# Row sums of the attention taken in halves of the queries, with four exponential buffers that change roles and one output buffer

## The reference

```python
h = layernorm(x) * (scale + 1) + shift          # shift, scale, gate from silu(cond) @ mod_w + mod_b
q, k, v = heads(h @ w_qkv)
q, k = rope(layernorm(q) * q_norm_w), rope(layernorm(k) * k_norm_w)
attn = softmax(q @ k.T / sqrt(32))
out = x + (concat_heads(attn @ v) @ w_out) * gate
```

## Time and profile before

| | |
|---|---|
| three runs | 1780.75, 1782.88 and 1783.54 us, median 1782.88 us |
| the profiled execution | 1788.56 us, its span 1786.7 us |
| TensorE clock granted, mean over the span | 0.980 of full speed |
| busy: PE, DVE, ACT, POOL | 94%, 70%, 58%, 36% of the span |
| chain that ended last | PE 85%, ACT 7%, DVE 5%, issue 2%, DMA 1% |
| main loop, tiles in flight (107 to 1637 us) | nearly all steps alike, 26.17 us in the one shown |

### The profile page before, as it was taken

One profiled execution on the slowest core, in us unless ns is written; L12 is line 12 of the kernel. 1 busy time (PEld: TensorE's weight loads), 2 busy tenths in 40 slices (PEclk: granted clock), 3 DMA queues, 4 the chain that ended last, 5 costly groups with the idle time before them and its releaser, 6 DMA issues.

```text
span 1786.7 us, 32167 instructions
## 1 busy us (share of the span) xinstructions
PE 1685.0 (94%) x12334; PEld 981.8 (55%) x12334; DVE 1243.3 (70%) x1605; ACT 1035.4 (58%) x1547; POOL 634.4 (36%) x707
## 2 busy tenths in 40 slices
PE   6978899999999999999999999999999999998777
PEld 3644455555555555555555555555555555554334
DVE  8766667767777776777777677777767777775443
ACT  3445656666666666666656656666665666665452
POOL 0513234334433433443343343334334333433222
PEclk9989999999999999999999999999999999999888
DMA  6034455546555564654546465464645546454544
GB/s 208 25 66 89 96 117 118 130 98 134 118 107 131 116 133 96 136 115 107 133 110 135 99 133 116 107 136 110 130 104 130 121 102 139 107 114 94 112 106 119
DMA packets 55566, 205.38 MB, mean 115 GB/s; under 512 B 6888, under 2 KB 6888, under 8 KB 39160
## 3 DMA queue, kind: packets, MB, share of 16 engines
q0 software_dynamic: 18288, 133.18, 39.0%
q1 hardware_dynamic: 37128, 70.14, 11.7%
HBM read 53.25 MB, written 16.88 MB: 39 GB/s over the span
## 4 chain that ended last, share of the span: by engine, by line
PE 85%; ACT 7%; DVE 5%; issue 2%; DMA 1%; SPq 0%; DVEq 0%; ACTq 0%
PE SA L413 13%; PE Y L325 11%; PE Y L338 10%; PE Y L328 9%; PE Y L332 9%; PE MB L441 7%; ACT probs L751 7%; PE O L432 7%; PE SM L381 7%; PE MB L360 3%; PE SA L417 3%; DVE cst L994 2%; PE SA L315 1%; PE SA L391 1%; PE SM L413 1%
## 5 line engine op out<-in xcount | busy, mean ns | idle before, releaser
L994 DVE TENSOR_REDUCE cst<-SM 128x2 fp32r<-128x1024 f32 x256 | 313.5, 1225 | 346.8 <-PE MB L381 346.8
L751 ACT ACTIVATE probs<-SM 128x1024 f32<-128x1024 f32 x256 | 262.0, 1023 | 242.1 <-PE SM L417 240.9
L1216 POOL DMA_DIRECT2D probs<-probs x127 | 110.2, 868 | 820.8 <-ACT probs L753 759.3
L994 DVE TENSOR_REDUCE cst<-MB 128x2 fp32r<-128x1024 f32 x256 | 311.4, 1217 | 0.0
L432 PE MATMUL O<-probs,vals 128*32 128x512 f32 x2048 | 278.1, 616 | 0.0
L753 ACT ACTIVATE probs<-SA 128x1024 f32<-128x1024 f32 x256 | 261.0, 1020 | 0.0
L651 ACT ACTIVATE rows<-Y 128x512 f32<-128x512 f32 x121 | 72.3, 597 | 268.0 <-PE Y L332 268.0
L325 PE MATMUL Y<-wqkv_hi,hT_hi 128*128 128x512 f32 x716 | 214.0, 420 | 0.0
L328 PE MATMUL Y<-wqkv_hi,hT_lo 128*128 128x512 f32 x716 | 193.1, 391 | 0.5 <-DVE hT_lo L976 0.5
L381 PEld LDWEIGHTS SM<-qk_hi 32*128 32x128 f32 x512 | 51.2, 183 | 258.9 <-issue 78.3
L332 PE MATMUL Y<-wqkv_lo,hT_hi 128*128 128x512 f32 x716 | 191.7, 389 | 0.0
(11 more groups left out here) (205 smaller groups left out, 3466.4 us busy)
## 6 DMA issues: line engine op xcount, KB each, us to landing
probs<-probs POOLq DMA_DIRECT2D x127, 1024.0 KB, 7.7
xin<-in_x_dram SPq DMA_DIRECT2D x62, 256.0 KB, 6.8
xres<-in_x_dram SPq DMA_DIRECT2D x60, 256.0 KB, 2.6
out_dram<-xres SPq DMA_DIRECT2D x60, 256.0 KB, 3.7
shift_scale<-mod_rows SPq DMA_DIRECT2D x15, 512.0 KB, 6.0
gate<-mod_rows SPq DMA_DIRECT2D x16, 256.0 KB, 5.2
rows<-in_L_cond_mod_w_dram SPq DMA_DIRECT2D x2, 1024.0 KB, 8.8
probs<-in_L_cond_w_qkv_dram SPq DMA_DIRECT2D x2, 1024.0 KB, 13.2
```

The source lines that it names most:

```text
L751: act.activation(probs[:, a, 2:4, :], SM[:], ACT.Exp).then_inc(s_exp, 1)
L994: dve.tensor_reduce(heads[:, 2 * half:2 * half + 2, 0], bank[:], AX.X, ALU.max, negate=True).then_inc(max_out, 1)
L1216: pool.dma_start(probs[:, probs_buffer(t - 1)].rearrange("p h n -> p (h n)"), probs[:, probs_buffer(t)].rearrange("p h n -> p (h n)"), acc ...
```

## The change

The exponentials get a fourth buffer, and which buffer a quarter uses alternates from group to group (`probs_buffer`). The products with ones are split into halves of 256 queries, and one half is done in each quarter, in front of `weigh_values`: of the first sum in quarter 3 and in quarter 0 of the next step, of the second in quarters 1 and 2 of the next step. They go to bank Y, between the projections, in place of MB, and the waits on PE, ACT and DVE follow. `log_sums`, `inverse_sums` and with them `scale_o` come a quarter later, `output_high` comes last in the step, and POOL's order changes. The outputs of all batch elements share one buffer in two layouts, so that a group of one element overwrites a tile of the last. `w_out` is loaded into the fourth exponential buffer, and its high and low parts are made ahead of the loop.

```diff
-    def probs_buffer(t):
-        return 1 if t % 2 else t
+    def probs_buffer(g, t):
+        return t ^ (g % 2)
...
-        probs = sb("probs", [P, 3, HG, T])
+        probs = sb("probs", [P, 4, HG, T])
...
-        oT = sb("oT", [P, 2, NG, T])
+        oT = sb("oT", [P, NG, TT, P])
...
-        wout_raw = oT[:, 1]
+        wout_raw = probs[:, 3]
...
+        def group_out(g):
+            return oT[:, :, g % NG, :] if (g // NG) % 2 else oT[:, g % NG, :, :]
+        def tile_out(n):
+            return oT[:, n % TT, :, :] if (n // TT) % 2 else oT[:, :, n % TT, :]
+        def half_cols(h):
+            return slice(h * T // 2, (h + 1) * T // 2)
...
-                if t == 1 and g >= 2:
-                    pe.wait_ge(sum_added, g - 1)
-                if t == 3 and g >= 1:
-                    pe.wait_ge(first_summed, g)
...
-            def add_over_keys(g, t, bank):
+            def add_over_keys(g, t, h):
                 pe.wait_ge(first_added if t == 0 else second_added, 16 * (g + 1))
+                if h == 1 or t == 2:
+                    pe.wait_ge(first_summed, 2 * g + (1 if t == 0 else 2))
+                if h == 1 and t == 2:
+                    pe.wait_ge(sum_added, 2 * g + 1)
+                if t == 0 and h == 0 and g > 0:
+                    pe.wait_ge(sum_added, 2 * g)
+                cols = half_cols(h)
                 for i in range(HG):
-                    mm = pe.matmul(bank[head_rows(i), :], ones_r[:, 0:E].bitcast(F32), probs[:, t, i, :],
+                    mm = pe.matmul(Y[head_rows(i), cols], ones_r[:, 0:E].bitcast(F32),
+                                   probs[:, probs_buffer(g, t), i, cols],
                                    start=True, stop=True, skip_group_check=True)
                 mm.then_inc(ones_done, 1)
...
                 scores_by_key(s, 0)
                 if s > 0:
+                    if tile(s + 5):
+                        pe.wait_ge(raw_out, raw_count(s + 5, 1))
+                    add_over_keys(s - 1, 0, 1)
                     weigh_values(s - 1, 3)
                 if group(s + 1):
                     scores_by_query(s + 1, 0)
                 if s > 0 and tile(s + 4):
-                    if tile(s + 5):
-                        pe.wait_ge(raw_out, raw_count(s + 5, 1))
-                    else:
-                        pe.wait_ge(y_gated, s - 5)
+                    pe.wait_ge(first_summed, 2 * s)
                     project(s + 4, 2, Y[:])
                 scores_by_key(s, 1)
                 if s > 0:
-                    if group(s + 1):
-                        pe.wait_ge(max_out, 2 * TT * (s + 1) + 2)
-                    add_over_keys(s - 1, 2, MB[:, 0, :])
+                    if tile(s + 4):
+                        pe.wait_ge(v_out, s + 5)
+                    add_over_keys(s - 1, 2, 0)
                 weigh_values(s, 0)
                 if group(s + 1):
                     scores_by_query(s + 1, 1)
...
                     if n == 0:
                         pe.wait_ge(wout_low, 1)
                     pe.wait_ge(o_low, n + 1)
-                    if tile(s + 4):
-                        pe.wait_ge(v_out, s + 5)
-                    else:
-                        pe.wait_ge(y_gated, n)
+                    pe.wait_ge(sum_added, 2 * s - 1)
                     project_out(n, Y[:], 0, 4)
                 if tile(s + 6):
                     transpose_x(s + 6)
...
                     project_out(n, Y[:], 4, 12)
                 scores_by_key(s, 2)
+                if s > 0:
+                    if n >= 0:
+                        pe.wait_ge(y_gated, n + 1)
+                    add_over_keys(s - 1, 2, 1)
                 weigh_values(s, 1)
                 if group(s + 1):
                     scores_by_query(s + 1, 2)
                 if tile(s + 6):
-                    if s - 5 >= 0:
-                        pe.wait_ge(y_gated, s - 4)
+                    if s > 0:
+                        pe.wait_ge(sum_added, 2 * s)
                     else:
                         pe.wait_ge(v_out, s + 5)
                     project(s + 6, 0, Y[:])
                 scores_by_key(s, 3)
                 if group(s + 1):
-                    pe.wait_ge(max_out, 2 * TT * (s + 1) + 6)
-                    add_over_keys(s, 0, MB[:, 0, :])
+                    if tile(s + 6):
+                        pe.wait_ge(raw_out, raw_count(s + 6, 0))
+                    add_over_keys(s, 0, 0)
                 weigh_values(s, 2)
                 if group(s + 1):
                     scores_by_query(s + 1, 3)
                 if tile(s + 6):
-                    pe.wait_ge(raw_out, raw_count(s + 6, 0))
+                    pe.wait_ge(first_summed, 2 * s + 1)
                     project(s + 6, 1, Y[:])
...
-                if g == NG:
-                    act.wait_ge(wout_low, 1)
-                if b > 1:
-                    act.wait_ge(o_low, TT * (b - 1))
-                act.activation(oT[:, b % 2, g % NG, :], O[:], ACT.Copy).then_inc(o_out, 1)
+                if b > 0:
+                    act.wait_ge(o_low, g - NG + 1)
+                act.activation(group_out(g), O[:].rearrange("p (t n) -> p t n", t=TT), ACT.Copy).then_inc(o_out, 1)
...
+            def move_first_sum(g, h):
+                act.wait_ge(ones_done, 4 * g + h + 1)
                 if g > 0:
                     act.wait_ge(o_scaled, g)
                 else:
                     act.wait_ge(parts_out, 3)
-                act.activation(sum_inv[:], MB[:, 0, :], ACT.Copy).then_inc(first_summed, 1)
+                cols = half_cols(h)
+                act.activation(sum_inv[:, cols], Y[:, cols], ACT.Copy).then_inc(first_summed, 1)
...
+                    if g > 0:
+                        act.wait_ge(pv_step, TT * (g - 1) + (t ^ 1) + 1)
                     if t == 0:
                         if g > 0:
-                            act.wait_ge(ones_done, 2 * g - 1)
+                            act.wait_ge(first_added, 16 * g)
                         else:
                             act.wait_ge(w_low[0], 1)
+                    elif t == 1:
+                        if g > 0:
+                            act.wait_ge(ones_done, 4 * g - 2)
+                        else:
                             act.wait_ge(w_low[1], 1)
-                    elif t == 1 and g > 0:
-                        act.wait_ge(pv_step, n - 1)
-                        act.wait_ge(second_added, 16 * g)
                     elif t == 2:
                         if g > 0:
-                            act.wait_ge(ones_done, 2 * g)
+                            act.wait_ge(second_added, 16 * g)
                         else:
                             act.wait_ge(mod_partial, 3)
                     elif t == 3:
-                        act.wait_ge(pv_step, n - 1)
-                        act.wait_ge(first_added, 16 * (g + 1))
-                a = probs_buffer(t)
+                        if g > 0:
+                            act.wait_ge(ones_done, 4 * g)
+                        else:
+                            act.wait_ge(wout_low, 1)
+                a = probs_buffer(g, t)
...
+            act.wait_ge(ld_wout, 16)
+            act.activation(wout_hi[:], wout_raw, ACT.Copy).then_inc(wout_high, 1)
...
                 key_exponentials(s, 0, 0)
+                if s > 0:
+                    move_first_sum(s - 1, 1)
                 key_exponentials(s, 0, 1)
+                if s > 0:
+                    move_o(s - 1)
                 if tile(s + 5):
                     square(s + 5, 1)
-                if s > 0:
-                    move_o(s - 1)
                 if s > 0 and tile(s + 4):
                     move_v(s + 4, Y[:])
                 key_exponentials(s, 1, 0)
                 key_exponentials(s, 1, 1)
-                if s > 0:
-                    log_sums(s - 1, sum_inv[:])
-                    inverse_sums(s - 1)
                 if tile(s + 6):
                     x_high(s + 6)
                 if tile(s + 5):
...
                 key_exponentials(s, 2, 0)
                 key_exponentials(s, 2, 1)
-                if s - 4 >= 0:
-                    output_high(s - 4)
-                if s == 1:
-                    act.wait_ge(ld_wout, 16)
-                    act.activation(wout_hi[:], wout_raw, ACT.Copy).then_inc(wout_high, 1)
+                if s > 0:
+                    log_sums(s - 1, sum_inv[:])
+                    inverse_sums(s - 1)
                 if tile(s + 6):
                     move_qk(s + 6, 0, Y[:])
                 key_exponentials(s, 3, 0)
                 if s < LAST:
-                    move_first_sum(s)
+                    move_first_sum(s, 0)
                 key_exponentials(s, 3, 1)
+                if s - 4 >= 0:
+                    output_high(s - 4)
...
+            def add_sums(g, h):
+                dve.wait_ge(ones_done, 4 * g + 3 + h)
+                dve.wait_ge(first_summed, 2 * g + 1 + h)
+                cols = half_cols(h)
```

(25 more changed lines are left out.)

64 lines of the change are left out of this document (30 added, 34 removed).

## The result

Over six runs of each kernel, the changed one takes 1788.79 us median (1787.44 to 1791.63), the one before 1782.92 (1780.75 to 1784.02): ratio 1.0031, 95% interval 1.0018 to 1.0043. It is slower by 0.3%; 1779.5 was forecast.

A forecast was written before the change was run, and what follows sets the result against it. PE was taken to bound the kernel, stopped by late exponentials. Held steps -1.6, ten free steps -5.5 and the end +4 gave -3: 1785.5 profiled, 5.7 lower for the median, stated as 1779.5 us; range 1753 to 1798.

The forecast's parts named there:

- The halves: Products with ones on PE: a half costs 0.46 us, a quarter 2.58, saving 0.55 us a step.
- the free step: Steps 1 to 4 and 57 to 62, without `normalize_x` and `add_residual` together: 25.62 us each.
- The rivals at 0.50 and 0.60: Dearer half products on PE: 0.50 us each gives 1786 us, chance 0.08; 0.60 gives 1800, chance 0.12.
- The place and time of the meeting: At a step's end DVE's `normalize_x` begins at 5.40 us after quarter 3's first matmul, inside POOL's `add_residual`.
- They take turns: DVE and POOL alternate whole instructions at a step's end: L960 ends at 6.57 us, `output_low` 7.71, L963 8.25.
- POOL is not interrupted: Rival: `output_low` also goes ahead of DVE's L960; DVE done at 8.60, step 26.49 us, total 1798, chance 0.10.
- the held step: Steps 5 to 56, where PE waits 0.52 us for `low_qk`: 26.14 us each, 0.03 below before.
- the way from L987 to PE's start: DVE work of 0.59 us, `low_qk` 1.41 and an assumed 0.1 for the semaphore: PE can go on at 10.35.
- PE's own arrival: PE itself would reach the next step's `scores_by_query` 9.83 us after quarter 3's first matmul.
- The term of -1.6: The 52 steps 5 to 56, at -0.03 us each.
- Free steps and end: Ten steps gain 0.55 us each, -5.5; in the last step `project_out(59)` waits 3.0 more, clock 3, taken as +4.
- The edits costed at nothing: Adding DMA, half copies, `add_sums`, `scale_o`, xres store, output parts and `w_out` copies: taken as covered, 0 us.

The follow-up runs named there:

- set_ahead: The changed kernel with a one-column memset, waited for, between POOL's adding DMA and `add_residual`: 1780.16 us, ratio 0.998 to the kernel before.
- wait_between: The changed kernel with one more wait on POOL, `output_low` waiting for the `add_residual` before it: 1771.41 us, ratio 0.993 to the kernel before.
- res_early: The changed kernel with `add_residual` moved from the end of POOL's step to ahead of the rotations: 1749.9 us, ratio 0.980 to the kernel before.

## Why the prediction failed

- **The halves: right.** 0.46 forecast, 0.46 and 0.45 measured (809.16 to 809.62, 828.18 to 828.63), and 0.456 in the mean of all from 250 to 1560 us; quarters 2.57 for 2.58, the free step 25.58 for 25.62. The rule of the Trainium skill, "TensorE: Matmul & The Clock Gate", section "Wait — 56ns, not 53.3ns?", would give 8 x 62 ns = 0.50; these rows give 57 ns a matmul and speak against its applying here. The rivals at 0.50 and 0.60 fall.
- **The place and time of the meeting: right, in part by luck.** From the first matmul of quarter 3 (827.04): exponentials done 3.48 (3.48 forecast), the DMA at 3.78 (3.92), `add_residual` done at 5.97 (6.02), L984 begun at 5.39 (5.40). But `add_residual` began 0.60 behind the DMA, not 0.82, and took 1.59, not 1.28: two errors that cancel. The 0.82 of the earlier trace rows was a wait. `scale_o` stood there until ACT had the inverse sum, at 818.80, and began 0.09 later:

```profile
818.17 0.63 ACT L726 ACTIVATE sum_inv<-sum_inv 128x512 f32<-128x512 f32 x1
```

- **"They take turns": this step failed.** L984 was to end at 6.57 and did at 7.76; `output_low` was to end at 7.71 behind it and did at 7.20 ahead of it; L987 was done at 8.55, not 8.25. This is the rival "POOL is not interrupted", given 0.10, which had 8.60. Its case against was rows 6 and 7; but there POOL's two instructions stand with a gap of 0.08 between them (87.93 + 0.73 to 88.74), far from a DMA, and in the code the second waits for the first's result (`rotate`). `set_ahead` shows that what decides is the DMA right in front, `wait_between` that a wait inside the pair undoes it. The row that would have warned was not in the trace of before: no such pair stood behind a DMA.
- **What that cost.** `low_qk` ended 10.46 after quarter 3 (836.10 + 1.40) for 10.25. PE waited 0.64 for 0.52, and the held step was 26.24 for 26.14: 0.10 x 52 = 5 us. That it was no more is luck. `wait_between`, where DVE has its turn, shows what the forecast's own mechanism gives, with one more wait on POOL: L987 is done 2.81 after L984 begins (2.85 forecast), and the step is 25.93, not 26.14. So the missing turn cost 0.31 a step, 16 us, and 11 of them had been put on already by small terms set too dear: the way from L987 to PE's start, and PE's own arrival. The rival, with 0.87 of wait and a step of 26.49, put too much on: DVE's two steps between L987 and `low_qk` took 0.51 for 0.59, and PE went on 0.05 after `low_qk` (811.25 to 811.30) where 0.1 was assumed.
- **The held step of before: read too long.** One step of 26.17 was taken for all. The mean over steps 5 to 56 is 26.11. 0.06 x 52 = 3 us. The term of -1.6 was really +6.9 over these 52 steps.
- **Free steps and end: right in size, the free steps in part by luck.** -5.3 for -5.5 and +3.5 for +4. In the -5.3 stand +1.5 for step 57, with its wait of 1.99, and -2.1 for step 59, where the kernel before had the lower granted clock (0.88 against 0.93). At the end the forecast names 3.0 of wait and 3 for the clock and takes 4 without saying how; measured are 2.98 of wait and 1.2 for the clock. The cause of the end was half right: `output_high` is as late as said, but POOL's `scale_o` chain is as late too, and the forecast did not name it. The edits costed at nothing cost nothing: no wait of PE on bank Y for a copy stands in the list, and the first L400 (before: L391) is at 95.98 in both kernels.
- **The sum.** -3 became +5.9 in the medians: 5 from the turn (16, less the 11), 3 from the step of before, 1 for the rest. These are errors of 0.2% to 0.3% on a forecast whose two large terms, -29 of halves and +27 of meeting, nearly cancel. The chance of slower, 0.35, was too low for that: 0.03 a step of margin is below what either term was known to.

That a meeting can hold a whole instruction is stated by the Trainium skill, "SBUF — State Buffer", section "SBUF: two separate sides": the pair of ports that the two engines share is an exclusive lock held for a whole instruction, also against DVE operations with two SBUF inputs. The 0.54 to 0.56 from POOL's end to DVE's, as worked out above for four kernels, agree. That the wait can last over two instructions, 2.37 in place of 0.74, these runs show.

## What to carry to other kernels

When a product hides a wait in some stretches and is missing in others, splitting it evenly pays (26.10 to 25.58 us a step here, once nothing else was in the way), but every queue that the edit reorders has to be laid over the other engine that shares its port: a pair put behind a DMA cost all of it. A gap between two starts is a cost only if nothing was waited for in it. If two large terms of a forecast cancel, take the mean of many steps for both, not one step, and put the chances at even. When the queue's order is free, try first to move the short instructions of the other engine to where it does not meet: one moved call was worth about 2%.

## What the runs showed of the hardware

- Right behind a DMA that POOL issues, two instructions with no wait in front are recorded 0.3 longer (1.56 to 1.59 for 1.28) and overlap by 0.33, and a DVE instruction with two SBUF inputs that waits gets no turn between them. It does with an instruction waited for after the DMA, or with a wait between the two. Behind the DMA of the earlier trace rows, where the next instruction still waited for ACT, it is not so: that one took 1.35. What happens inside POOL in those 0.3 is not shown; that it has already begun the second is our reading.
- DVE can be kept out before the record of POOL's instruction begins: in step 56 L984 began 0.37 ahead of `add_residual` and took 3.71; with the memset in front it took 0.74, as it did 0.39 behind the start of the DMA alone in the kernel before (1590.12 in its timeline).
- The memset and its wait put the recorded start of `add_residual` 0.47 later (1.07 behind the DMA's for 0.60), its end only 0.17. So most of the 0.3 in the longer record was not work; that it was a wait inside POOL is our reading too.
- A DVE instruction of 33 columns took 1.19 beside `add_residual` and 0.20 in the changed kernel, where they no longer met (822.11 in its timeline); in `res_early`, where they meet again, 1.20.
